# Keys and values of three attention layers formed one stage earlier and kept in DRAM

## The reference, cut to what matters

```
for layer in range(4):
    q = layernorm(x) @ Wq + bq          # [4, 512, 256], 16 heads of 16 (layers 1 to 3), 1 head (layer 4)
    k = ctx @ Wk + bk                   # [4, 1601, 256]
    v = ctx @ Wv
    (layer 2: rotary turn of q and k, halves of each head swapped)
    x = x + tanh(g) * (softmax(mask(q k^T * scale)) @ v @ Wo + ...)
    x = x + tanh(g') * ffn(layernorm(x))   # quantised linear; experts, top 1, relu; experts, gelu; experts, top 2, selu
```

## Time and profile before

| what | value |
|---|---|
| time, median of 3 (lowest to highest) | 4374.93 us (4374.8 to 4383.88) |
| profiled execution: time, span | 4381.18 us, 4380.0 us |
| PE busy | 3603.8 us, 82% of the span |
| DVE busy | 2138.6 us, 49% |
| ACT busy | 2104.0 us, 48% |
| POOL busy | 737.1 us, 17% |
| mean granted clock of PE | 0.916 |
| DMA | 323.62 MB, mean 74 GB/s |

### The profile page before, as it was taken

The page is one execution under the profiler, slowest core; times in us unless marked ns, Lnnn a source line. Parts: engine busy times, 40 slices in busy tenths (PEclk is TensorE's granted clock), DMA queues, the critical chain, the costliest instruction groups (busy, mean ns, idle before and its releaser), DMA issues. The chain is left out here.

```text
span 4380.0 us, 54568 instructions
## 1 busy us (share of the span) xinstructions
PE 3603.8 (82%) x19622; PEld 1953.4 (45%) x19622; DVE 2138.6 (49%) x3325; ACT 2104.0 (48%) x4606; POOL 737.1 (17%) x764
## 2 busy tenths in 40 slices
PE   3999999965698989896865989898959698893993
PEld 2334343343242424233862434343339366593993
DVE  4766666646656565673016666666530211242332
ACT  1566666631365555563322666666723222251662
POOL 1111121013060505101120212030010200003103
PEclk8999999987899999997987999999969799996997
DMA  6242415013515151502546151515034100122555
GB/s 131 42 61 45 68 46 69 1 56 85 72 54 61 60 67 58 68 1 97 181 148 98 38 68 39 68 46 60 1 132 166 57 15 15 45 69 95 182 182 107
DMA packets 215237, 323.62 MB, mean 74 GB/s; under 512 B 40034, under 2 KB 156195, under 8 KB 214587
## 3 DMA queue, kind: packets, MB, share of 16 engines
q1 hardware_dynamic: 185754, 215.00, 24.8%
...
## 5 line engine op out<-in xcount | busy, mean ns | idle before, releaser
L631 DVE TENSOR_REDUCE mxp<-m 128x1 f32<-128x802 f32 x1536 | 1454.4, 988 | 730.2 <-PE m L731 728.1
L839 ACT ACTIVATE e_t<-s 128x512 f32<-128x512 f32 (+1 forms) x2496 | 1361.6, 599 | 734.1 <-PE s L750 732.6
L731 PE MATMUL m<-kaug,qaug 97*128 97x401 bf16 x3072 | 801.6, 343 | 221.4 <-DMA kaug<-maskrow 132.4
L750 PE MATMUL s<-qaug,kaug 100*128 100x512 bf16 (+1 forms) x2496 | 873.7, 387 | 20.6 <-ACT e_t L839 11.8
L761 PE MATMUL pv<-e_t,v 128*32 128x512 f32 (+1 forms) x4992 | 673.4, 612 | 0.2
L750 PEld LDWEIGHTS s<-qaug,kaug 100*128 100x128 bf16 (+1 forms) x2496 | 237.4, 101 | 700.0 <-ACT e_t L839 457.2
L731 PEld LDWEIGHTS m<-kaug,qaug 97*128 97x128 bf16 x3072 | 281.9, 100 | 594.1 <-DVE mxp L631 164.1
L1642 PE MATMUL y<-w,hT 128*128 (+1 forms) x1504 | 346.8, 385 | 11.7 <-DVE hT L1499 11.7
L1633 PE MATMUL h<-xtT,w 128*128 128x128 f32 x2496 | 297.5, 278 | 10.9 <-DMA w<-in_L_w 7.3
L1642 PEld LDWEIGHTS y<-w,hT 128*128 128x128 f32 x1504 | 283.2, 193 | 48.9 <-issue 6.4
L1633 PEld LDWEIGHTS h<-xtT,w 128*128 128x128 f32 x2496 | 290.9, 195 | 12.2 <-issue 12.0
(11 more groups left out here) (274 smaller groups left out, 3480.4 us busy)
## 6 DMA issues: line engine op xcount, KB each, us to landing
...
```

What stands on the lines that cost most here:

```text
L631: dve.tensor_reduce(a.mxp[:, u.g % 2, half, n:n + 1], a.m_slot[u.m % 2][:].rearrange("p (a n) -> p a n", a=2)[:, :, 0:PIECE + 1], AX.XY, A ...
L731: m = pe.matmul(slot[:, 512 * k:512 * k + PIECE + 1], a.qaug[0:R_MAX, u.g, j, P * qc:P * qc + P], a.kaug[0:R_MAX, u.g, j, k0:k0 + PIECE + ...
L750: pe.matmul(slot[0:KW[u.k], :], a.kaug[0:R_ALL, u.g, u.j, P * u.k:P * u.k + KW[u.k]], a.qaug[0:R_ALL, u.g, u.j, :], start=True, stop=True) ...
L839: act.activation(a.e_t[0:KW[u.k], e % 2, u.j, :], a.s_slot[u.s % 3][0:KW[u.k], :], ACT.Exp).then_inc(s_free.sem, 1)
```

## The change

Keys and values of layers two to four are formed in the feed-forward stage of the layer before, from a new helper `Prepared`, and written to DRAM as float32 (`keys` [4, 256, 1601], `values` [4, 128, 13, 256]). The 16 chunks of the four batches are cut into parts, and PE and ACT run a part at marked places of the stage: in the quantised stage one chunk before the norm, one behind it, one behind each rotation and each product, and seven at the end; with experts one before the norm, six after the rank matmuls, nine after the last tile. ACT copies each unit out of PSUM and issues its store itself. SP loads the context four chunks ahead. In the quantised stage the rotation has one PSUM slot in place of two.

In layers two and three the attention no longer has key and value units on PE and ACT. SP loads a key unit from DRAM into the buffer of the set (`split_at`), POOL or DVE splits it with the first part made there too, and SP stores the parts as before; values of a batch are two loads. The order of the units is a new one, `lay_out_ready`: in batch 0 the key splits stand before the norm for PE and ACT, q after it (POOL splits q in layer two, DVE in layer three), then all fetches; in later batches the projection is 6 steps over the attend of group 1 and 6 over jobs 0 to 36 of the attend of group 2, and in layer two every third split goes to DVE. In layer two the turned keys come from copies within DRAM with the halves of each head swapped (`turned`), those of batch 0 first, those of batches 1 to 3 behind the first loads, all issued by SP. The mask row of a group is one DMA in place of four. Layer four loads keys and values of a batch with three DMAs into two buffers.

```
+class Prepared:
+        self.w, self.slots = w, slots
+        self.wk, self.wv, self.bk = sb("p_wk", [P, DC, D]), sb("p_wv", [P, DC, D]), sb("p_bk", [P, DC])
+        self.at, self.kf = sb("p_ctx", [P, 4, DC, 512]), sb("p_kf", [P, 3, 512])
+        self.vb = sb("p_vb", [P, 2, 4, D])
+        self.chunks, s, k = [], 0, 0
+        for b in range(B):
+            for n_c, (c0, n) in enumerate(CHUNKS):
+                c = dict(b=b, n_c=n_c, i=len(self.chunks), keys=[], values=[])
+                for j in range(DC):
+                    c["keys"].append((j, s, k))
+                    s, k = s + 1, k + 1
+                for t in range(c0 // P, -(-(c0 + n) // P)):
+                    c["values"].append((t, s))
+                    s += 1
+                c["end"] = s
+                self.chunks.append(c)
+        self.n, self.n_keys = s, k
+        self.parts, first = [], 0
+        for n in counts:
+            self.parts.append(self.chunks[first:first + n])
+            first += n
+        self.parts.append(self.chunks[first:])
+        self.loaded = 0
...
+def prepare_sp(kn, p, upto):
+    sp, p_full = kn.nc.sync, kn.sema("p_full")
+    for c in p.chunks[p.loaded:upto]:
+        f, (c0, n) = c["i"] % 4, CHUNKS[c["n_c"]]
+        arrived = kn.sema(f"p_ctx{f}", DMA)
+        if c["i"] >= 4:
+            sp.wait_ge(p_full.sem, p_full.at(p.chunks[c["i"] - 4]["end"]))
+        sp.dma_start(p.at[:, f, :, 0:n],
+                     p.w["ctxT"][c["b"], :, c0:c0 + n].rearrange("(c p) n -> p c n", p=P)).then_inc(arrived.sem, DMA)
+        p.loaded += 1
...
+def prepare_pe(kn, p, part):
+    pe, p_full, p_free, p_w = kn.nc.tensor, kn.sema("p_full"), kn.sema("p_free"), kn.sema("p_w", DMA)
+    many = len(p.slots)
+    pe.wait_ge(p_w.sem, p_w.at(3))
+    for c in p.parts[part]:
+        f, (c0, n) = c["i"] % 4, CHUNKS[c["n_c"]]
+        arrived = kn.sema(f"p_ctx{f}", DMA)
+        pe.wait_ge(arrived.sem, arrived.at(c["i"] // 4 + 1))
+        for j, s, _ in c["keys"]:
+            if s >= many:
+                pe.wait_ge(p_free.sem, p_free.at(s - many + 1))
+            for kc in range(DC):
+                m = pe.matmul(p.slots[s % many][:, 0:n], p.wk[:, kc, P * j:P * j + P], p.at[:, f, kc, 0:n],
+                              start=kc == 0, stop=kc == DC - 1)
+            m.then_inc(p_full.sem, 1)
+        for t, s in c["values"]:
+            if s >= many:
+                pe.wait_ge(p_free.sem, p_free.at(s - many + 1))
+            k0 = P * t - c0
+            for kc in range(DC):
+                m = pe.matmul(p.slots[s % many][0:KW[t], 0:D], p.at[:, f, kc, k0:k0 + KW[t]], p.wv[:, kc, :],
+                              start=kc == 0, stop=kc == DC - 1)
+            m.then_inc(p_full.sem, 1)
...
+def prepare_act(kn, p, part):
+    act, p_full, p_free, p_w = kn.nc.scalar, kn.sema("p_full"), kn.sema("p_free"), kn.sema("p_w", DMA)
+    keys, values = kn.dram["keys"], kn.dram["values"]
+    many = len(p.slots)
+    act.wait_ge(p_w.sem, p_w.at(3))
+    for c in p.parts[part]:
+        c0, n = CHUNKS[c["n_c"]]
+        for j, s, k in c["keys"]:
+            kept = kn.sema(f"p_k{k % 3}", DMA)
+            act.wait_ge(p_full.sem, p_full.at(s + 1))
+            if k >= 3:
+                act.wait_ge(kept.sem, kept.at(k // 3))
+            act.activation(p.kf[:, k % 3, 0:n], p.slots[s % many][:, 0:n], ACT.Identity,
+                           bias=p.bk[:, j:j + 1]).then_inc(p_free.sem, 1)
+            act.wait_ge(p_free.sem, p_free.at(s + 1))
+            act.dma_start(keys[c["b"], P * j:P * j + P, c0:c0 + n], p.kf[:, k % 3, 0:n]).then_inc(kept.sem, DMA)
+        f = c["i"] % 2
+        kept = kn.sema(f"p_v{f}", DMA)
+        if c["i"] >= 2:
+            act.wait_ge(kept.sem, kept.at(c["i"] // 2))
+        for i, (t, s) in enumerate(c["values"]):
+            act.wait_ge(p_full.sem, p_full.at(s + 1))
+            act.copy(p.vb[0:KW[t], f, i, :], p.slots[s % many][0:KW[t], 0:D]).then_inc(p_free.sem, 1)
+        h, t0 = KW[t], c["values"][0][0]
+        act.wait_ge(p_free.sem, p_free.at(s + 1))
+        act.dma_start(values[c["b"], 0:h, t0:t + 1, :], p.vb[0:h, f, 0:t + 1 - t0, :]).then_inc(kept.sem, DMA)
...
+    def lay_out_ready(self):
+        lead, n = self.lead, 0
+        self.add("begin", b=0, what="kvq")
+        for n_c in range(len(CHUNKS)):
+            for c in range(DC):
+                self.split("k", 0, c, n_c, ("pool",) if n < (4 if self.rope else 5) else ("dve",))
+                n += 1
+        self.add("ln")
+        for c in range(DC):
+            self.split("q", 0, c, 0, ("pool",) if self.rope else ("dve",))
+        for g in range(NG):
+            self.add("fetch", b=0, g=g, what="k", k=1, by=f"kd{g}")
+            if g == 0:
+                self.add("fetch", b=0, g=0, what="q", k=NG, by="qd")
+        for _ in self.maxima(0, 0):
+            pass
+        self.add("bias")
+        for g in range(NG):
+            self.add("take", b=0, g=g)
...
+            projected = self.chain(self.project(b + 1, ("pool", "pool", "dve") if self.rope else ("pool",), "kvq"),
+                                   *(self.then("fetch", b=b + 1, g=g, what="kq", k=1, by=f"kd{g}") for g in (0, 1)))
+            self.attend(1, b, peaks, (projected, 6, 0, JOBS - 1), (self.normalise(0, b), 2, 2 * HG, JOBS - 1))
+            self.attend(2, b, peaks, (projected, 6, 0, 36), (self.normalise(1, b), 2, 2 * HG, JOBS - 1))
...
+def head_ready_sp(kn, a, n_of):
+    def load(x):
+        c0, n = CHUNKS[x.k]
+        arrived = sig(f"kl{x.f}", DMA)
+        if x.before:
+            sp.wait_ge(split[x.before.by].sem, split[x.before.by].at(x.before.n + 1))
+        sp.dma_start(a.split_at[x.f][0][:, 0:n], keys[x.b, P * x.j:P * x.j + P, c0:c0 + n]).then_inc(arrived.sem, DMA)
+        n_of(f"kl{x.f}")
+        if rope:
+            if x.j == 0 and x.k == 0:
+                sp.wait_ge(swapped.sem, swapped.at(2 * x.b + 2))
+            sp.dma_start(a.split_at[x.f][1][:, 0:n], turn_keys[x.b, P * x.j:P * x.j + P, c0:c0 + n]).then_inc(arrived.sem, DMA)
+            n_of(f"kl{x.f}")
...
+    for u in plan.units:
+        if u.kind == "begin":
+            ks = of_batch("k", u.b)
+            if u.b:
+                for by, n in set(a.arrived.values()):
+                    sp.wait_ge(sig(by, DMA).sem, sig(by, DMA).at(n))
+            elif rope:
+                for k in range(2):
+                    sp.dma_start(halves(turn_keys[0], k), halves(keys[0], 1 - k)).then_inc(swapped.sem, DMA)
+                    n_of("swapped")
+            ahead = 2 if u.b else 3
+            for x in ks[0:ahead]:
+                load(x)
+            if rope:
+                for n_c, (c0, n) in enumerate(CHUNKS):
+                    tables.append((("k", u.b, n_c), (n_c + 1) % 2, c0, n, [x for x in ks if x.k == n_c]))
+                tables.append((("q", u.b, 0), 1, 0, T, of_batch("q", u.b)))
+                next_table()
+            if u.b == 0:
+                for t, src in ((a.wq, row(w["wq"])), (a.bq, w["bq"])) + (((a.wqr, row(w["wqr"])), (a.bqr, w["bqr"])) if rope else ()):
+                    sp.dma_start(t[:], src).then_inc(ld.sem, DMA)
+                    n_of("ld")
+                for t, src in ((a.woa, w["woa"]), (a.bva, w["bva"]),
+                               (a.bob, w["bo"].rearrange("(a n) -> a n", a=1).to_broadcast([P, D]))):
+                    sp.dma_start(t[:], src).then_inc(ld.sem, DMA)
+                    n_of("ld")
+                sp.wait_ge(filled.sem, filled.at(1))
+                for t, n in ((a.kaug, S2), (a.qaug, T)):
+                    ones = a.fill[0:R_ALL - R_MASK, 0:n]
+                    sp.dma_start(t[R_MASK:R_ALL, :, :, :].rearrange("p g j n -> p (g j) n"),
+                                 ones.rearrange("p (a n) -> p a n", a=1).to_broadcast([R_ALL - R_MASK, H, n])).then_inc(rows.sem, DMA)
+                    n_of("rows")
+                sp.wait_ge(filled.sem, filled.at(2))
+                if rope:
+                    for b in range(1, B):
+                        for k in range(2):
+                            sp.dma_start(halves(turn_keys[b], k), halves(keys[b], 1 - k)).then_inc(swapped.sem, DMA)
+                            n_of("swapped")
+            else:
+                sp.wait_ge(v_taken.sem, v_taken.at(NG * u.b))
+            sp.dma_start(a.vn[:, 0:KT - 1, :, :, :].rearrange("p k g j d -> p k (g j d)"),
+                         values[u.b, :, 0:KT - 1, :]).then_inc(vl.sem, DMA)
+            sp.dma_start(a.vn[0:KW[-1], KT - 1, :, :, :].rearrange("p g j d -> p (g j d)"),
+                         values[u.b, 0:KW[-1], KT - 1, :]).then_inc(vl.sem, DMA)
+            n_of("vl")
...
+        elif u.kind in ("q", "k"):
+            if u.j == 0 and u.kind == "k":
+                next_table()
+            c0, n = CHUNKS[u.k] if u.kind == "k" else (0, T)
+            dst = w["kparts"] if u.kind == "k" else w["qparts"]
+            sp.wait_ge(split[u.by].sem, split[u.by].at(u.n + 1))
```

(53 more changed lines are left out.)

359 lines of the change are left out of this document (218 added, 141 removed).

## The result

| | us |
|---|---|
| before, median of 4 runs | 4377.7 (4374.8 to 4383.9) |
| after, median of 4 runs | 4409.6 (4404.8 to 4430.8) |
| ratio, 95% interval | 1.008 (1.005 to 1.011) |
| forecast | 4318 (4235 to 4385) |

Busy time by stage in the changed kernel's profiled execution (span 4429.5, before 4380.0), with the columns of the earlier trace rows: quantised stage, layer two, its experts, layer three, its experts, layer four.

A forecast was written before the change was run, and what follows sets the result against it. TensorE was taken to bound the attentions of layers two to four and to wait in the feed-forward stages between. The terms -88 - 46 - 45 + 66 + 56 = -57 gave 4324 profiled, 4318 us as median, range 4235 to 4385.

The forecast's parts named there:

- Layer four, -88: Layer four's attention: 23.0 us of projection a batch vanish, about 1 us of wait replaces it; 88 us less, bounds 68 to 90.
- The wait for kaug: Second attends, layers two and three: still end on kaug's fetch, 20 us behind q's split; layer three's wait 8 to about 14.
- Layer three, -46: Layer three's attention: first attends 19 us shorter, second about 3 longer, first batch plus 5; 46 us less in all.
- Layer two, -45: Layer two's attention: first attends 17 us shorter, second plus 1, first batch plus 3; 45 us less in all.
- TensorE has two maxima in hand and stops for the rest, 6.5 us, about twice a batch: 13 of the 29 come back: Layer two's first attends: DVE splits of 8.5 us stop TensorE; of 29.2 us projection removed, 17 are left as gain.
- The first batch: Layer two's first batch: first maxima at about 110 us against 106 before, plus 3; bounds -12 to +35.
- (b): Rival, SP's queue: slow swap copies within DRAM delay layer two's first maxima by 100 us, about 4416 us; chance 0.07.
- Second and third attends: Layer two: the second attend still ends on kaug's fetch, at 52.5 us against 51.2, plus 1.
- Quantised stage, +66: Layer one's quantised stage: takes layer two's projections, 90 us of TensorE; 154 us against 88.3, bounds +50 to +85.
- Experts, +56: Experts of layers two and three: plus 3 up to the tiles, plus 24.4 behind them, 27 each; bounds 40 to 75.
- (a): Rival: the attentions give all their projection back; about 4166 us, 4242 for half of the difference; chance 0.22.
- (c): Rival, the tails: ACT sets the pace, chunks of 9 instead of 6.9 us; plus 75, about 4393 us; chance 0.07.

The follow-up runs named there:

- wide_only: Changed kernel with only layer four's keys and values formed ahead, layers two and three as in the kernel before: 4339.2 us, 0.989 of before.
- q_first: Changed kernel with q's splits ahead of the key splits in batches 1 to 3 and the projection ended earlier: 4337.2 us in its repeat.
- pool_only: Changed kernel with all splits of layer two's batches 1 to 3 on POOL, none on DVE: 4376.7 us in its repeat.
- early_dve: The kernel early, but with every third split of layer two given to DVE again: 4324.4 us.
- late_swaps: Changed kernel with the swap copies for batches 1 to 3 issued one batch at a time, behind the last fetch of the batch before: 4409.2 us.
- after_3: The changed kernel unaltered, run again in a later round: median 4389.1 us, 1.003 of before.
- early: Changed kernel with next batch's key units begun in attend 0, batches 1 to 3's splits all on POOL, swap copies one batch at a time: 4240.5 us, 0.967.

## Why the prediction was wrong, step by step

The forecast missed the median by 92 us. By the profiles the steps missed by 107: the profiled execution of the changed kernel lies 21 us above its median, where the forecast took off 6. Of its two signs of being wrong (no wait for kaug, or first maxima of layer two later than 130 us) neither came: the wait stayed in five of the six second attends, and the maxima came at 126.5. The signs watched other places than those that failed.

**Layer four, -88: right** (-91.3; alone with its experts stage, wide_only measured what the profile says).

**The wait for kaug: right in place, and not in size.** The second attends took 72, 67, 76 and 62, 59, 61 us, forecast 69 and 61, and part of that agreement is luck, most of all where layer two's second wait was 0.8 us and a stop for DVE stood in its place. In layer three the wait was to grow from 8 to about 14 us and was 8.6, 8.6 and 7.7. The rest of the length is a second wait near the attend's end, 4.0, 1.8 and 3.4 us for the transfer of the row maxima (`qaug<-tm`), which is issued behind 24 fetches in SP's queue, and slower matmuls behind both.
```profile
2668.80 0.85 PE L1032 MATMUL m<-kaug,qaug 97*128 97x401 bf16 x2 [8.55 <-DMA kaug<-maskrow]
...
2684.56 0.61 PE L1051 MATMUL s<-qaug,kaug 100*128 100x512 bf16 x1 [3.97 <-DMA qaug<-tm]
```
q_first shows what both hang on: with q first and the projection ended earlier they are gone.

**Layer three, -46: right in the main** (-37.6). Of the 8 us, 5 are the first attends: 42.1 us, not 40.5. The 40.5 of the earlier trace rows is an attend of layer one; a plain attend of layers two and three took 42.1 before the change too. Another 5 are the third attends (44.7, 42.1 and 44.8 us), whose matmuls run slower behind the wait for `qaug<-tm`. The first batch and the second attends gave 2 back.

**Layer two, -45: this failed** (+11.1). Three sub-steps did:
- "TensorE has two maxima in hand and stops for the rest, 6.5 us, about twice a batch: 13 of the 29 come back". All three first attends together fell by 26 us, not by 51. The stops themselves were nearly right. TensorE was idle for 17.4, 18.7 and 11.1 us in the three (length less busy time), which is 41 us more than in three plain attends of 2.0 each; 39 were forecast. A split took 5.1 to 10.9 us, 7.6 in the mean, where 8.5 was taken. **What failed is a term put at nothing: a stop costs TensorE speed behind it.** The same 238 matmuls kept it busy for 45.3, 48.6 and 44.6 us at a clock of 0.84, 0.80 and 0.88, and in a plain attend for 40.06 us at 1.00: 18 of the missing 25 us. Of the other 7, 2 are the stops, 2 the plain attend (42.1, not 41.4) and 2 a rounding (16 of the 29 were left, 17 taken). I had also left out nm, for which the longest stop, 11.7 us, waited with no maxima in hand. pool_only shows the cause: without DVE's splits 40 us come back. early_dve prices them at 17 us a batch.
- The first batch, "about 110. Plus 3": 126.5 us, plus 20.5. I priced the swap copies by their bandwidth, 6.5 MB in 32 us, and that was no worse than taken (329 to 343 GB/s of all traffic in the windows below). But I placed them beside the splits, where they stand ahead of table, loads and stores of the same queue and hold each; late_swaps gives 15 back. It is the place in the queue that my rival (b) named, at a sixth of its price and without its low bandwidth.
```profile
1114.00:1125.00 11.00, 4.41 (x8) 1.45 (x7) 0.00 (x0) 0.00 (x0) 5.29 (x5) 0.81 0.97 329
1125.00:1135.00 10.00, 0.00 (x0) 0.00 (x0) 0.00 (x0) 0.00 (x0) 0.13 (x1) 0.50 0.97 343
```
- Second and third attends +10 and +6, forecast +3 and 0. The forecast had DVE's stops in the first attends alone; in batches 2 and 3 one of the q splits was DVE's too, in the second attend, and TensorE stopped behind it for 6.4 and 4.5 us. The wait for kaug was 14.6, 0.8 and 13.0 us (13.4, 13.3 and 13.4 before), that for `qaug<-tm` 3.7, 3.5 and 3.1 (1.2, 1.3 and 0 before). The third attends were no longer idle than before (2 us each) but busy for longer, at 0.93 to 0.96.

**Quantised stage, +66: right** (+70.6). **Experts, +56: mis-sized** (+95.3). Up to the last matmul of the tiles a stage was to cost 3 and cost 15, and the nine chunks behind it were to take 46.2 us and took 54 and 56. The hole before the first tile of layer two:
```profile
2148.75 6.02 PE L218 MATMUL h<-p_ctx,p_wk 128*128 128x512 f32 x8
...
2176.96 1.58 PE L226 MATMUL h<-p_wv,p_ctx 128*128 128x256 f32 x4 [3.06 <-ACT p_kf L243]
2179.62 6.00 PE L218 MATMUL h<-p_ctx,p_wk 128*128 128x512 f32 x8 [1.08 <-issue]
...
2196.43 0.66 PE L1984 MATMUL b<-ident,xt 128*128 128x128 f32 x4 [0.46 <-ACT p_vb L253]
```
Six chunks took 47 us, not 36: the first and, behind a stop of 3 us beside the scatter, the fifth hold their keys at 6.0 us where 3.6 is the price at full clock, and the chunk ahead of the norm put everything 5 us later. In the rounds where these stops were short or absent the six took 38 to 42 and the nine 46 to 48; in after_3 the two stages cost 33 and 31. The forecast's 27 to 29 was near the better kind, and some 30 us of the 39 missed here go with the round.

**Rivals.** (a) was the strongest statement of what the change makes possible, and early came to 4240, near its 4242 for half of the difference: the attentions give their projection back when the places of q and of the splits are changed too. (c) was wrong: behind the tiles most full chunks kept TensorE's 6.9 us, and the nine took 54 us by single stops (2.5 and 2.4 us in layer two's experts), not by ScalarE's pace. What spoke for a loss and had only 0.16 was the sum of small ones.
